# First feed-forward block: two VectorE passes of the 4-bit rounding replaced by two ScalarE passes, its additions issued one pair later, and the last turning steps placed between score units

## The reference, cut to what matters

```python
BLOCK = 16
_GRID = [0.0, 0.5, 1.0, 1.5, 2.0, 3.0, 4.0, 6.0]
def fp4_quant_dequant(x):                      # blocks of 16 along the last dimension
    scale = jnp.maximum(jnp.max(jnp.abs(xb), axis=-1, keepdims=True) / 6.0, 1e-12)
    xn = xb / scale
    q = _GRID[searchsorted(_MID, abs(xn))] * sign(xn) * scale
def fp4_linear(x, w):
    return einsum('bsk,nk->bsn', fp4_quant_dequant(x), fp4_quant_dequant(w))
gate = fp4_linear(x, w_gate)
y = fp4_linear(x, w_up)
h = silu(gate) * y                             # 4 x 512 x 352
return fp4_linear(h, w_down)
...
scores = einsum('bhqd,bhkd->bhqk', qh, kh) + mask     # second layer's attention, 16 heads, 77 keys
weights = softmax(scores)
```

## Time and profile before

| | us |
|---|---|
| median of 3 runs | 800.57 (800.1 to 802.02) |
| the profiled execution's time | 803.98 |
| its span, first to last instruction | 802.2 |
| VectorE busy | 527.0 (66%) |
| TensorE busy | 632.1 (79%) |
| ScalarE busy | 325.9 (41%) |
| GpSimd busy | 276.9 (35%) |

### The profile page before, as it was taken

One profiled execution on the slowest core, in us unless ns is written; L12 is line 12 of the kernel. 1 busy time (PEld: TensorE's weight loads), 2 busy tenths in 40 slices (PEclk: granted clock), 3 DMA queues, 4 the chain that ended last, 5 costly groups with the idle time before them and its releaser, 6 DMA issues.

```text
span 802.2 us, 10170 instructions
## 1 busy us (share of the span) xinstructions
PE 632.1 (79%) x3016; PEld 391.4 (49%) x3016; DVE 527.0 (66%) x1380; ACT 325.9 (41%) x627; POOL 276.9 (35%) x562
## 2 busy tenths in 40 slices
PE   5667877537899999898788871387788798989997
PEld 3334333334765564564334430243344576667875
DVE  8684636998762553378526557773567779788664
ACT  3042555124324334264153340315455364545553
POOL 4342354211240312115441621303222345545453
PEclk9795988777899999799899995589998999999999
DMA  8864421002205323002354320224300324324351
GB/s 261 181 170 132 83 58 55 1 0 66 66 12 146 93 42 87 9 19 75 105 146 144 58 79 0 67 69 119 125 4 1 88 85 121 112 87 123 103 132 53
DMA packets 67990, 67.73 MB, mean 84 GB/s; under 512 B 25119, under 2 KB 48223, under 8 KB 67552
## 3 DMA queue, kind: packets, MB, share of 16 engines
q1 hardware_dynamic: 61326, 64.61, 29.9%
q10 hardware_dynamic: 6610, 2.47, 1.2%
HBM read 50.29 MB, written 17.60 MB: 85 GB/s over the span
## 4 chain that ended last, share of the span: by engine, by line
PE 37%; DVE 21%; issue 13%; POOL 12%; DMA 9%; ACT 4%; SPq 4%; POOLq 0%; ACTq 0%; DVEq 0%
POOL sg L705 9%; PE ps L1784 7%; PE ps L1724 5%; PE ps L1764 5%; DVE mraw L1342 3%; DMA QG<-q_parts 3%; DMA q_parts<-loT 2%; PE ps L1675 2%; PE ps L1950 2%; PE ps L1686 2%; PE ps L1941 1%; SPq L327 1%; PE ps L1669 1%; PE ps L1768 1%; PE ps L1767 1%
## 5 line engine op out<-in xcount | busy, mean ns | idle before, releaser
L795 ACT ACTIVATE PT<-ps 110x512 f32<-110x512 f32 x192 | 111.2, 595 | 140.7 <-PE ps L1764 68.0
L1342 DVE TENSOR_REDUCE mraw<-ps 128x4 f32<-128x308 f32 x256 | 116.3, 475 | 78.8 <-PE ps L1724 33.9
L1724 PE MATMUL ps<-KG,QG 98*128 98x308 f32 x256 | 107.6, 440 | 47.7 <-DVE mraw L1342 25.6
L705 POOL TENSOR_TENSOR sg<-sg,cb 128x512 f32<-128x512 f32 x64 | 84.4, 1322 | 74.9 <-ACT sg L968 74.9
L1764 PE MATMUL ps<-QG,KG 128*110 128x512 f32 x192 | 92.6, 500 | 13.3 <-ACT PT L795 10.6
L1724 PEld LDWEIGHTS ps<-KG,QG 98*128 98x128 f32 x256 | 53.0, 211 | 89.9 <-DVE mraw L1342 59.6
L585 POOL TENSOR_TENSOR nt<-nhv,rs 128x4 f32<-128x4 f32 (+1 forms) x84 | 18.1, 216 | 175.2 <-DVE rs L1084 143.1
L1571 DVE TENSOR_TENSOR ps<-ps,sg 128x512 f32<-128x512 f32 x72 | 50.3, 698 | 39.5 <-POOL sg L705 36.6
L1784 PE MATMUL ps<-PT,VN 128*18 128x512 f32 x512 | 72.4, 639 | 0.0
L1764 PEld LDWEIGHTS ps<-QG,KG 128*110 128x110 f32 x192 | 34.6, 184 | 57.2 <-ACT PT L795 43.0
L968 ACT ACTIVATE sg<-ps 128x512 f32<-128x512 f32 x72 | 43.0, 597 | 44.8 <-PE ps L2012 44.2
(11 more groups left out here) (304 smaller groups left out, 1427.2 us busy)
## 6 DMA issues: line engine op xcount, KB each, us to landing
cb<-c_parts SPq DMA_DIRECT2D x64, 256.0 KB, 3.3
QG<-q_parts SPq DMA_DIRECT2D x48, 256.0 KB, 4.0
KG<-k_parts SPq DMA_DIRECT2D x48, 154.0 KB, 3.1
q_parts<-hiT SPq DMA_DIRECT2D x14, 256.0 KB, 2.0
q_parts<-loT SPq DMA_DIRECT2D x14, 256.0 KB, 2.0
k_parts<-kmH SPq DMA_DIRECT2D x16, 154.0 KB, 2.4
k_parts<-kmL SPq DMA_DIRECT2D x16, 154.0 KB, 2.8
VN<-v_parts SPq DMA_DIRECT2D x16, 144.0 KB, 2.8
```

Source lines behind the costliest of these rows:

```text
L705: pool.tensor_tensor(sg[:, n % 3, :], sg[:, n % 3, :], cb[:, k % CRING, :], ALU.mult).then_inc(sc_done, 1)
L795: act.activation(PT[0:w, q % PTR, :], ps[0:w, 4 + q % 2, :], ACT.Exp, scale=SCALE[l]).then_inc(exp_done, 1)
L1342: dve.tensor_reduce(mraw[:, n % 2, i, g * HG:(g + 1) * HG], ps[:, u % 2, 0:GK].rearrange("p (h k) -> p h k", k=K), AX_X, ALU.max).then_inc ...
L1724: ins = pe.matmul(o, QG[0:KS, n % 3, g, q], KG[0:KS, n % 3, g, :], start=True, stop=l not in (1, 2))
```

## The change

Seven edits, all in the first feed-forward network and its end:

1. The factor 1 - 2^-22 was multiplied into the inverse scales by L1006. Now the multiplication by the inverse scale carries it, as a SCALAR_TENSOR_TENSOR in place of a TENSOR_TENSOR, for the eight pairs and for `quantise_batch`.
2. The constant of the rounding (L998) is made for the pairs by two ScalarE instructions, `steps(j)`: Relu(w * c - c), then + c, with c = 1.5 * 2^22 and the two biases in a new tile `magic`. VectorE raises `h_bits` after the exponent bits; ScalarE raises `h_steps`.
3. `rounded(j)` is split. `scaled(j)` (scales, multiplication, exponent bits) stays in iteration j; the addition and the subtraction, still called `rounded`, follow one pair later, behind `scaled(j+1)`. `multiply(j)` waits for them as before. `hscale` gets a third buffer.
4. On ScalarE `steps(j-1)` stands behind `silu(2j+1)` and ahead of `normalise_out` and the `hT_out` of the same iteration.
5. TensorE's iteration 9 is gone: its `turn(14)`, `turn(15)` and the last three `down` stand between score units 2 and 9.
6. VectorE does `rounded(7)` behind `q_rest(1)`, ahead of the first maximum.
7. Two small memsets fill `magic` ahead of `product(0)`.

```diff
+            def steps(j):
+                w = qh[:, j % 2, 1, :]
+                act.wait_ge(h_bits, j + 1)
+                act.activation(w, w, ACT.Relu, bias=magic[:, 0:1], scale=1.5 * 2.0 ** 22).then_inc(h_steps, 1)
+                act.wait_ge(h_steps, 2 * j + 1)
+                act.activation(w, w, ACT.Identity, bias=magic[:, 1:2]).then_inc(h_steps, 1)
...
                     if j < T // 2:
                         silu(2 * j)
                         silu(2 * j + 1)
+                    if j <= T // 2:
+                        steps(j - 1)
                     if j == 3:
                         normalise_out((1, B - 1))
...
             def quant_steps(w, src, inv):
-                link(dve.tensor_tensor(w[0], src, inv, ALU.mult))
+                link(dve.scalar_tensor_tensor(out=w[0], in0=src, scalar=1.0 - 2.0 ** -22, in1=inv, op0=ALU.mult, op1=ALU.mult))
...
+            def scaled(j):
+                link(dve.tensor_scalar(s, s, 1.0 / 6.0, 1e-12, ALU.mult, ALU.max))
+                link(dve.reciprocal(qs[:, 1, :], s))
                 if j >= 2:
                     dve.wait_ge(hq_done, j - 1)
+                link(dve.scalar_tensor_tensor(out=w[0], in0=v, scalar=1.0 - 2.0 ** -22, in1=qs[:, 1, :].unsqueeze(2).to_broadcast([P, 44, 16]),
+                                              op0=ALU.mult, op1=ALU.mult))
+                dve.tensor_scalar(w[1].bitcast(I32), w[0].bitcast(I32), EXP_BITS, None, ALU.bitwise_and).then_inc(h_bits, 1)
             def rounded(j):
-                link(quant_scales(hscale[:, j % 2, :], qs[:, 1, :]))
-                quant_steps(w, v, qs[:, 1, :].unsqueeze(2).to_broadcast([P, 44, 16])).then_inc(hq_scaled, 1)
+                dve.wait_ge(h_steps, 2 * j + 2)
+                link(dve.tensor_tensor(w[0], w[0], w[1], ALU.add))
+                dve.tensor_tensor(w[0], w[0], w[1], ALU.subtract).then_inc(hq_scaled, 1)
...
-                    rounded(j)
+                    scaled(j)
+                    rounded(j - 1)
...
                 q_rest(1)
+                rounded(T // 2 - 1)
...
-                    if j == T // 2 + 1:
-                        pe.wait_ge(silu_done, T)
-                        for u in range(2 * TPB):
-                            scores(0, u // G, u % G)
...
-                down(T - 1)
-                for u in range(2 * TPB, 4 * TPB):
+                pe.wait_ge(silu_done, T)
+                for u in range(4 * TPB):
                     scores(0, u // G, u % G)
+                    if u == 2:
+                        turn(T - 2)
+                    if u == 4:
+                        down(T - 3)
+                        turn(T - 1)
+                    if u == 6:
+                        down(T - 2)
+                    if u == 8:
+                        down(T - 1)
```

More of the change, by code:

```diff
@@ L839, in attention @@
                             silu(c // 3 + 1)
+                        if k == B and l == 0 and c == 6:
+                            steps(0)
                         if c == 5 and 1 <= k <= last:
@@ L1125, in quantise_batch @@
                 link(dve.tensor_reduce(s[0], v, AX_X, ALU.max, apply_absolute_value=True))
-                link(quant_scales(s[0], s[1]))
+                link(dve.tensor_scalar(s[0], s[0], 1.0 / 6.0, 1e-12, ALU.mult, ALU.max))
+                link(dve.reciprocal(s[1], s[0]))
                 link(quant_steps(w, v, s[1].unsqueeze(2).to_broadcast([P, 32, 16])))
@@ L1303, in product @@
                 dve.wait_ge(h_done, j + 1)
+                if j >= 3:
+                    dve.wait_ge(hq_done, j - 2)
+                link(dve.tensor_reduce(hscale[:, j % 3, :], h.rearrange("p t (n e) -> p (t n) e", e=16), AX_X, ALU.max,
+                                       apply_absolute_value=True))
+            def scaled(j):
+                v = fh[:, j % 3, :, :].rearrange("p t (n e) -> p (t n) e", e=16)
+                w = [qh[:, j % 2, i, :].rearrange("p (b e) -> p b e", e=16) for i in range(2)]
+                s = hscale[:, j % 3, :]
+                link(dve.tensor_scalar(s, s, 1.0 / 6.0, 1e-12, ALU.mult, ALU.max))
+                link(dve.reciprocal(qs[:, 1, :], s))
                 if j >= 2:
                     dve.wait_ge(hq_done, j - 1)
-                link(dve.tensor_reduce(hscale[:, j % 2, :], h.rearrange("p t (n e) -> p (t n) e", e=16), AX_X, ALU.max,
-                                       apply_absolute_value=True))
+                link(dve.scalar_tensor_tensor(out=w[0], in0=v, scalar=1.0 - 2.0 ** -22, in1=qs[:, 1, :].unsqueeze(2).to_broadcast([P, 44, 16]),
+                                              op0=ALU.mult, op1=ALU.mult))
+                dve.tensor_scalar(w[1].bitcast(I32), w[0].bitcast(I32), EXP_BITS, None, ALU.bitwise_and).then_inc(h_bits, 1)
             def rounded(j):
-                v = fh[:, j % 3, :, :].rearrange("p t (n e) -> p (t n) e", e=16)
-                w = [qh[:, j % 2, i, :].rearrange("p (b e) -> p b e", e=16) for i in range(2)]
-                link(quant_scales(hscale[:, j % 2, :], qs[:, 1, :]))
-                quant_steps(w, v, qs[:, 1, :].unsqueeze(2).to_broadcast([P, 44, 16])).then_inc(hq_scaled, 1)
+                w = [qh[:, j % 2, i, :] for i in range(2)]
+                dve.wait_ge(h_steps, 2 * j + 2)
+                link(dve.tensor_tensor(w[0], w[0], w[1], ALU.add))
+                dve.tensor_tensor(w[0], w[0], w[1], ALU.subtract).then_inc(hq_scaled, 1)
                 dve.wait_ge(hq_scaled, j + 1)
@@ L1384, in after @@
                     if c == 3 and l == 0 and k == B:
+                        link(dve.memset(magic[:, 0:1], -1.5 * 2.0 ** 22))
+                        link(dve.memset(magic[:, 1:2], 1.5 * 2.0 ** 22))
                         product(0)
-                        rounded(0)
+                        scaled(0)
                     if c == 9 and k == 0 and l == 0:
@@ L1906, in ffn0 @@
                 input_transposed(1)
-                for j in range(2, T // 2 + 2):
+                for j in range(2, T // 2 + 1):
                     if j in (3, 5):
```

8 lines of the change are left out of this document (5 added, 3 removed).

## The result

The changed kernel took 804.98 us (median of 20 runs, 799.05 to 810.81) against 801.66 us (20 runs, 797.22 to 805.31) for the kernel before: ratio 1.005, 95% interval 1.0031 to 1.0068. By the ratio it is 4.0 us slower, 2.5 to 5.5 by the interval; the two medians are 3.3 us apart. The forecast was +5.4 us.

A forecast was written before the change was run, and what follows sets the result against it. VectorE looked like the bound, but the path product, two `up`, silu was as long, so late additions and queued copies would cost. Station shifts ran to +5.4 us at M16, kept to the end: 800.6 + 5.4 = 806.0 us, range 801.0 to 810.

The forecast's parts named there:

- VectorE's saving: VectorE's work in the network: 0.70 us less per pair, 0.16 per `quantise_batch`, 5.9 us in all if VectorE bounds everywhere.
- P1: Start of the second product: 1.7 us earlier, not 2.55, since its matmuls end only at 136.27.
- ScalarE's price: The two `steps` passes on ScalarE: 0.88 us each, 1.81 per pair with a handover, against 0.56 on VectorE.
- P2: Start of the third product: 2.6 us earlier, at 151.1.
- P3: Start of the fourth product: waits 3.6 us behind `turn(0)`, middle between clock levels, at 160.7, shift +0.4 us.
- P4: Start of the fifth product: residual 10.1 us after the fourth, a third of the way to low level; shift +3.8 us.
- P5: Start of the sixth product: chain from `quantise_batch(3)` unchanged, VectorE's saving turns into wait; shift +3.6 us.
- P6: Start of the seventh product: `turn(8)` needs pair 4's additions, 8.8 us to the residual against 7.32; shift +5.1 us.
- M0: First score maximum: 10.5 us after the eighth product against 7.32, 12.6 at low level; shift +7.6 us.
- M16: First maximum of the next batch: 13.1 us after the first maximum against 15.35, a 3.40 us stall gone; shift +5.4.
- VectorE as the bound: Rival: VectorE bounds throughout, so shorter passes count and the kernel takes 793.4 us; chance 0.08.
- TensorE at the full level: Rival: same places wait but TensorE keeps its full clock; +1.6 us, 802.2, no measurable change; chance 0.14.

The follow-up runs named there:

- e5: The changed kernel with `steps(j-1)` ahead of `silu(2j)` on ScalarE, additions still one pair late; 1.0057 of the kernel before.
- e9: The changed kernel with pair 0's additions directly behind product 1 and `steps(1)` behind both copies of iteration 2, nothing else altered; 1.0014 of the kernel before.
- e10: The changed kernel without edit 5: eight score units, the block of turns, eight units; 1.008 of the kernel before.
- e4: The changed kernel with the additions of pair j-1 directly behind the product of pair j on VectorE; 1.007 of the kernel before.
- e8: The changed kernel with unused bf16 matmuls as fillers where TensorE waits, ahead of turns 0, 3, 5 and 12; 1.0043 of the kernel before.
- e2: The changed kernel with the rounding's constant back on VectorE, no ScalarE `steps`, additions still one pair late; 1.0067 of the kernel before.
- e12: The kernel of e8 (changed kernel with filler matmuls where TensorE waits) run again; 1.0025 of the kernel before.
- e1: The kernel before with edit 5 alone, the last turns and downs spread between score units; 0.996 of the kernel before.
- e6: The changed kernel with additions directly behind the next product, copies ahead of `steps(1)`, later `steps(j-1)` ahead of the silus; 1.011 of the kernel before.

## Why the prediction was right, step by step

- **VectorE's saving.** Forecast 5.9 us, measured 6.6 less busy; that the two are close is in part chance. The multiplication did not rise to 0.97: L1334 takes 0.892, exactly the TENSOR_TENSOR's time. By durations L998 and L1006 give 5.7 us and the two batches 0.4. The other 0.5 was not forecast: the addition now belongs to the pair before, so it starts 0.44 us after the exponent bits (160.79 and 161.23), where L998 came 0.56 after them, and the two overlap in the trace. The 0.5 us that L1361 saves (see P1) and the 0.6 that L1341 loses once beside GpSimd cancel. A pair with nothing beside it is 5.74 us, not 5.96.
- **ScalarE's price.** Measured 0.875 and 0.882 us, against 0.88 forecast.
- **P1 and P2.** P1 came out to the digit by two errors that cancel. The projection's `yb` row stood 5.47 us after the first product and not 4.95, after a wait of 1.48. But the row behind it took 0.75 us and not the 1.25 of before, shown below, where it met GpSimd's multiplication (138.02 to 139.40), which the late additions moved away. In e5, e9 and e10 P1 is 8.06 to 8.20. P2 is 0.2 us earlier than forecast, since the multiplication did not rise and the pair is shorter.

```profile
138.69 1.25 DVE L1361 SCALAR_TENSOR_TENSOR x<-yb,tg,x 128x512 f32<-128x512 f32 x1
```

- **P3.** The middle between the levels was a fair guess (forecast 160.7 - 131.3 = 29.4, measured 29.66), but the size is luck: the granted clock rose in the middle of the two `up` here, and earlier in e10 (28.33). And the reason was half of it. I named only `turn(0)` behind the late additions. e4 showed a second tie, the copy behind `steps(1)`, which holds the same place to the same time. e9 shows the pair to be the cause, and e8 that 2.8 us of the wait need the low level too.
- **P4.** 10.07 us from product to residual against 10.1. The late additions alone hold it at 8.56, in e5 and e9 (9.19 in e2, whose additions come 0.6 later). The other 1.5 us are not the passes by themselves, since e9 has them in the same place. They are the passes and the low level together: in the changed kernel TensorE idled 3.29 us ahead of the second turn and most of the two `up` ran low (L1911 1.38 us for two matmuls), in e9 it idled 1.46 and they ran full (0.75). The first `up` began 4.73 us after P3, against 5.05 forecast. "A third of the way" to the low level was a guess that came out. The rows of the changed kernel:

```profile
161.04 0.52 PE L1921 MATMUL ps<-ident,fh 128*128 128x128 f32 x3 [3.29 <-ACT hqT L886]
163.16 1.38 PE L1911 MATMUL ps<-wqt,xnT 128*128 128x352 f32 x2
```

- **P5, P6.** 12.36 for P4 to P5 against 13.2 forecast, a matter of level: it is 13.4 in e5, e9, e10 and e12, with a granted clock of 0.53 to 0.58 in its last 5 us against 0.68. P5 to the residual 8.49 against 8.8.
- **M0.** 10.21 from P7 against 10.5; 11.4 to 11.6 in e5, e9 and e10, where the turns ran low. The forecast's figure holds for the full level, and the changed kernel's profile was a lucky one here.
- **M16.** This term was mis-sized: 11.94 and not 13.1. I took 16 units at 0.64 and added all the turning. With TensorE at the full level, as the 0.64 supposes, e1 and the changed kernel show that VectorE's pieces and maxima hide some 1.2 us of it. The forecast named only the 3.40 us gap at M8 as what goes; that before lost another 1.0 us to the low level in this stretch (e10) it did not see. The 1.2 us by which this term was too large are the largest part of the 1.9 by which the sum was too high at M16.
- **From M16 on.** That the shift stays to the end is not shown by the profiles, which differ by 7 us there for the same work. The ratio, 4.0 us against 3.5 at M16, agrees with it.
- **A reading.** The residual of before starts 0.1 us after `down(3)`, which ends at 166.91, and not 0.2; nothing hangs on it.
- **The rivals.** VectorE as the bound is refuted by 22 us of idle: the first `up` behind P2 starts 25.45 us after the first product, where this rival needed 22.4. TensorE at the full level was made in part in e8 and e12, which came to 1.0043 and 1.0025 with 1.3 us of the fillers' own delay in them; the rival, 802.2 us, is 1.002. So how much of the loss is the clock is not settled.

## What to carry to other kernels

When work is moved off the busiest engine, read what stands behind it on the engine that takes it, and what waits for a result that now comes later: here 6.6 us of busy time were taken away and 10.1 us of waiting came instead. Where several in-order queues pass one buffer round, a delay can have two ties of equal length, so loosing one shows nothing (e4, e5), and loosing both by one blanket rule may tie a third (e6); alter one place and read its station. An edit that only fills an idle stretch can be the whole gain of a bundle: edit 5 alone is 0.4% faster than before, and it hid part of the other edits' loss. When an engine's clock differs between two profiles, compare stretches at the same granted clock before you put a difference down to the order.

## What the runs showed of the hardware

- A SCALAR_TENSOR_TENSOR with a constant scalar costs what a TENSOR_TENSOR does: 0.892 us at 704 elements, 0.691 at 512, where the one with its scalar in a tile takes 0.752.
- A VectorE operation with two SBUF sources that meets GpSimd's 1.39 us TENSOR_TENSOR takes about 1.50 us instead of 0.89 (five times each in e4 and e6, L1341 once in the changed kernel); at 512 elements L1361 took 1.25 instead of 0.75 in before. Products with one source in PSUM that met it kept 0.89. In the row of e4 above GpSimd ended at 152.54 and VectorE at 153.28. The Trainium skill ("SBUF — State Buffer", Who interferes with whom) says that a VectorE instruction with two SBUF inputs and a GpSimd one that reads SBUF contend for a shared pair of ports, which one of them holds for its whole instruction while the other is blocked. An estimate by that page is that VectorE would have ended at 152.54 + 0.89 = 153.43, 0.15 us later than measured, so the rule gives nearly the size.
- Single executions of the same instructions differ by more than a us at one stretch where TensorE comes out of idling: P4 to P5 takes 11.99 us in e8 and 13.41 in e12 (granted clock 0.72 and 0.53 in its last 5 us), and P3 is at 29.66 in the changed kernel and at 28.33 in e10, whose code up to there is the same. A station of one profile is good to about that.
- Over a long stretch the same holds for the mean level: from M16 to the end, 574.7 to 576.0 us in the six profiles with a mean granted clock of 0.923 to 0.925 of full, 577.0 to 582.0 in the eight with 0.911 to 0.919.
